# Taps as matmuls, the skip term by scaled copies and flips, B and C of the first half chunk by matmuls, a new table of places

## The reference

```python
# 1: a state space layer, D_INNER 256, 16 states, 4 taps, rank 8
x_b, z = split(x @ W_in)                        # 256 and 256
xc = silu(conv_b + sum_k xpad[:, k:k + T] * conv_w[:, k])   # causal, 4 taps
proj = xc @ W_xproj                             # 40 columns: 8 delta, 16 B, 16 C
delta = softplus(proj[..., :8] @ W_dt + b_dt)
h = exp(delta * A) * h + delta * B * xc         # A = -exp(A_log), 16 states per channel
y = (sum_s h * C + D_param * xc) * silu(z)      # D_param * xc is the skip term
x = layernorm(x + y @ W_out)
# 2: retention between x (queries) and the context (keys, values)
x = layernorm(x + ((rot(x Wq) rot(ctx Wk)^T) * decay_mask) (ctx Wv))
# 3: 16 experts of 64 hidden units, the best 2 of each token, and a shared expert of 128
combine = softmax over the top 2 of (x @ router_w.T + router_bias), 0 elsewhere
x = layernorm(x + sum_e combine_e * (silu(x gate_e) * (x up_e)) down_e + shared(x))
```

## Time and profile before

| | |
|---|---|
| median of 3 runs | 1159.82 us (1152.06 to 1161.8) |
| the profiled execution | 1162.05 us, span of its instructions 1160.2 |
| mean granted TensorE clock | 0.965 of full |
| VectorE busy | 1064.0 (92%), 1492 instructions |
| TensorE busy | 1059.0 (91%), its weight loads 741.8 (64%) |
| ScalarE busy | 994.5 (86%) |
| GpSimd busy | 971.1 (84%) |
| largest groups | products with C 604.0, scans 595.3 on VectorE, decays 424.8, drives 328.4 |

### The profile page before, as it was taken

One profiled execution on the slowest core, in us unless ns is written; L12 is line 12 of the kernel. 1 busy time (PEld: TensorE's weight loads), 2 busy tenths in 40 slices (PEclk: granted clock), 3 DMA queues, 4 the chain that ended last, 5 costly groups with the idle time before them and its releaser, 6 DMA issues. The chain is left out here.

```text
span 1160.2 us, 18257 instructions
## 1 busy us (share of the span) xinstructions
PE 1059.0 (91%) x5831; PEld 741.8 (64%) x5831; DVE 1064.0 (92%) x1492; ACT 994.5 (86%) x2176; POOL 971.1 (84%) x590
## 2 busy tenths in 40 slices
PE   5677888999999999999999989999999999899998
PEld 2455665666767666666666657666666667666665
DVE  2999999999999999999999979999999999999532
ACT  5888898999989898999989879898999989898443
POOL 0587788989989898898989869898989988898844
PEclk9787999999999999999999989999999999999899
DMA  6543543555565544555554364554555655444212
GB/s 165 209 175 138 178 172 130 174 188 190 182 205 178 178 154 156 187 212 192 185 180 145 135 186 179 183 186 163 169 175 186 211 192 166 168 154 157 82 69 74
DMA packets 84111, 194.49 MB, mean 168 GB/s; under 512 B 17288, under 2 KB 47936, under 8 KB 67632
## 3 DMA queue, kind: packets, MB, share of 16 engines
q1 hardware_dynamic: 84016, 193.33, 48.8%
HBM read 179.14 MB, written 5.77 MB: 159 GB/s over the span
## 5 line engine op out<-in xcount | busy, mean ns | idle before, releaser
L934 POOL TENSOR_TENSOR read<-state,bc_all 128x1024 f32<-128x1024 f32 x256 | 604.0, 2363 | 130.4 <-DVE state L804 109.6
L804 DVE TENSOR_TENSOR_SCAN state<-decay,drive_bank 128x512 f32<-128x512 f32 (+1 forms) x464 | 595.3, 1315 | 0.4
L754 ACT ACTIVATE decay<-delta,a_neg 128x252 f32<-128x252 f32 x1024 | 424.8, 494 | 0.9
L796 DVE TENSOR_TENSOR drive_bank<-dx_bank,bc_all 128x512 f32<-128x512 f32 (+1 forms) x496 | 328.4, 701 | 3.3 <-issue 2.3
L371 PE MATMUL y_bank<-ident,read 128*128 128x128 f32 x2048 | 279.2, 281 | 30.9 <-POOL read L934 30.8
L371 PEld LDWEIGHTS y_bank<-ident,read 128*128 128x128 f32 x2048 | 240.1, 145 | 101.6 <-POOL read L934 58.1
L973 POOL TENSOR_TENSOR hid<-gu,comb_all 128x512 f32<-128x512 f32 (+1 forms) x136 | 164.8, 1212 | 17.3 <-DVE gu L895 13.8
L362 PEld LDWEIGHTS down_bank<-down_w,hid 128*128 128x128 f32 x1024 | 129.4, 192 | 38.3 <-issue 30.0
L362 PE MATMUL bank<-x2T,gate_w 128*128 128x512 f32 (+1 forms) x272 | 139.0, 603 | 9.4 <-ACT delta L734 3.9
L362 PE MATMUL down_bank<-down_w,hid 128*128 128x128 f32 x1024 | 134.9, 277 | 2.6 <-POOL hid L973 0.7
L362 PE MATMUL bank<-x2T,up_w 128*128 128x512 f32 (+1 forms) x272 | 132.9, 582 | 0.8 <-ACT xc L710 0.7
(11 more groups left out here) (128 smaller groups left out, 1384.7 us busy)
## 6 DMA issues: line engine op xcount, KB each, us to landing
bc_all<-bc_dram SPq DMA_DIRECT2D x128, 1024.0 KB, 5.4
comb_all<-comb_dram SPq DMA_DIRECT2D x240, 128.0 KB, 3.0
x_in<-in_x_dram SPq DMA_DIRECT2D x15, 256.0 KB, 5.7
ctx_in<-in_ctx_dram SPq DMA_DIRECT2D x15, 256.0 KB, 6.3
k_pair<-k_pair SPq DMA_DIRECT2D x30, 128.0 KB, 2.1
q_pair<-q_pair SPq DMA_DIRECT2D x30, 128.0 KB, 2.5
out_dram<-y_out SPq DMA_DIRECT2D x15, 256.0 KB, 3.1
comb_all<-comb_dram SPq DMA_DIRECT2D x32, 64.0 KB, 2.6
```

Source lines behind the costliest of these rows:

```text
L754: done = e.activation(seqs(decay_t[j % DECAYS][:, i, h, :])[:, :, 1:T], seqs(delta[c % 2][:, h, sub * SUB:(sub + 1) * SUB])[:, :, 1:T], AC ...
L796: e.tensor_tensor(drive_bank[:, a:b, :, :], dx_bank[:, :, :].unsqueeze(1).to_broadcast(shape), bc_all[group % BC_BUFS][:, 0, PAIR * i + a: ...
L804: e.tensor_tensor_scan(states(state_t[j % STATE_BUFS], a, b), states(decay_t[j % DECAYS], a, b), states(drive_bank, a, b), 0.0, ALU.mult, ...
L934: e.tensor_tensor(read_t[j % READS][:, :, :, :], state_t[j % STATE_BUFS][:, :, :, :], bc_all[group % BC_BUFS][:, 1, PAIR * i:PAIR * (i + 1 ...
```

## The change

What it does, part by part:

- Both halves of the convolution are four tap matmuls each, followed by silu with the bias (`xc`). The projection of half 1, the conv pass on ScalarE and the three taps on VectorE go. `w_tap` is made for both halves, from tap rows spread over all partitions (512 KB instead of 256).
- The skip term: ScalarE copies xc, scaled by D_param per channel, to `xd`, and TensorE adds it to `y_bank` by four transposes against the identity. `d_diag` goes.
- The weights W_dt are padded with zero rows from 8 to 40, so that delta is made from all 40 rows of `proj`.
- The first group of B and C is spread over the partitions by TensorE, a column of the identity repeated as weights, into `down_bank` and `y_bank`, and copied to `bc_all` by VectorE. The other groups go through DRAM as before.
- Start: the loads are spread over the queues of SyncE, ScalarE and GpSimd, many constants are loaded later, three activations on one column load function tables ahead of their use, `a_neg` is made on ScalarE, and for the first chunk VectorE copies `proj` and makes `dx_bank`.
- Last chunk: the combine weights are spread by 8 matmuls with a selector matrix, which VectorE makes behind its last scan, into `drive_bank`, `dx_bank` and `y_bank`; VectorE instead of GpSimd multiplies `hid`.
- `AT` and `EXP_AT` have five columns, for the first two chunks, the middle ones, the last but one and the last, and all places are new. `WHOLE_DRIVES` has four entries instead of one, `WHOLE_SCANS` four instead of three.

The diff, cut to its core:

```diff
+COLUMN = [3, 4] + [0] * (CHUNKS - 4) + [2, 1]
...
-    "tap_mm": [(-38, -40)],
-    "xb_mm": [(-43, -41)],
...
+    "weight_mm": [
+        (17, 129, -8, 6, 21), (12, 133, 11, 11, 1), (16, 133, -7, -21, 1), (14, 135, 17, 11, 4),
+        (12, 135, -7, -21, 1), (18, 135, -6, -1, 4), (2, 135, -7, 6, 11), (12, 135, -6, 6, -2)],
...
+    "tap_mm": [(-42, -40, -40, -61, -42), (-38, -38, -36, -46, -36)],
+    "xc": [(-36, -35, -36, -28, -44), (-34, -32, -32, -25, -43)],
+    "xd": [(1, 3, -7, -4, 3), (32, 25, 25, -1, 39)],
 }
-WHOLE_DRIVES = (7,)
-WHOLE_SCANS = (3, 6, 14)
+WHOLE_DRIVES = (3, 7, 8, 9)
+WHOLE_SCANS = (6, 7, 8, 9)
...
+        def last_weight(pair):
+
+            if pair < PAIR * HALVES:
+                return drive_bank[:, pair // HALVES, pair % HALVES, :]
+            return dx_bank[:, pair % HALVES, :] if pair < PAIR * HALVES + 2 else y_bank[:, pair % HALVES, :]
...
+                for c, h in due(tick, "tap_mm"):
+                    bank = take(("xb", c, h), tick, 3)
                     w.wait_ge(S["xT"], at(c))
-                    w.wait_ge(S["w_tap"], 1)
+                    w.wait_ge(S["w_tap"], h + 1)
                     for n in range(TAPS):
-                        done = mm(seqs(bank.t[:, 0:width(c)])[:, :, n:T], w_tap[:, TAPS - 1 - n, :],
+                        done = mm(seqs(bank.t[:, 0:width(c)])[:, :, n:T], w_tap[:, h, TAPS - 1 - n, :],
                                   seqs(xT[c % 3][:, 0:width(c)])[:, :, 0:T - n], start=n == 0, stop=n == TAPS - 1)
                     done.then_inc(S["tap_mm"], 1)
-                    bank.free = (S["xc"], at(c, 0, HALVES))
-                for c in due(tick, "xb_mm"):
-                    bank = take(("xb", c, 1), tick, 6)
...
+                    bank.free = (S["xc"], at(c, h, HALVES))
...
+                    if c == 0:
+                        for two in (0, 1):
+                            for pair in (0, 1):
+                                w.wait_ge(S["bc_copy"], 2 * two + pair - 1)
+                                for i in range(PAIR):
+                                    row = DT_RANK + GROUP * pair + PAIR * two + i
+                                    done = mm((down_bank, y_flat)[pair][:, i * SUB:(i + 1) * SUB],
+                                              ident[0:PROJ, row:row + 1].to_broadcast([PROJ, P]), proj[0:PROJ, 0:SUB])
+                                done.then_inc(S["bc_mm"], 1)
...
+                    mm(last_weight(pair), selector[0:EXPERTS, pair * P:(pair + 1) * P],
+                       combT[:, 0:SUB]).then_inc(S["weight_mm"], 1)
...
-                                mm(y_bank[:, q, h * P:(h + 1) * P], xc[c % 2][:, h, cols], d_diag[:, h, :],
-                                   start=h == 0 and q == 0, stop=False)
+                                flip(y_bank[:, q, h * P:(h + 1) * P], xd[:, h, q * P:(q + 1) * P],
+                                     start=h == 0 and q == 0, stop=False)
...
-                for c in due(tick, "conv_bias"):
-                    w.wait_ge(S["xb_mm"], at(c))
-                    w.wait_ge(S["xc"], at(c - 1, 1, HALVES))
-                    e.activation(conv[:, 0:width(c)], bank_of["xb", c, 1][:, 0:width(c)], ACT.Identity, bias=conv_b[:, 1:2],
-                                 scale=conv_w[:, 1, TAPS - 1:TAPS]).then_inc(S["conv_bias"], 1)
...
+                for c, sub in due(tick, "xd"):
+                    w.wait_ge(S["d_consts"], 16 * 2)
+                    w.wait_ge(S["xc"], at(c, 1, HALVES))
+                    w.wait_ge(S["y"], steps_before(c) + SUB_STEPS * (sub - 1) + 1)
+                    for h in range(HALVES):
+                        done = e.activation(xd[:, h, :], xc[c % 2][:, h, sub * SUB:(sub + 1) * SUB], ACT.Copy,
+                                            scale=d_param[:, h:h + 1])
+                    done.then_inc(S["xd"], 1)
...
-                for c in due(tick, "tap1"):
-                    tap(c, 1)
-                for c in due(tick, "tap2"):
-                    tap(c, 2)
-                for c in due(tick, "tap3"):
-                    tap(c, 3)
...
+                for c, pair in due(tick, "hid"):
+                    if c < LAST:
+                        continue
...
+                    e.tensor_tensor(hid[index % 3][:, 0:SUB], gu[index % 2][:, 0:SUB], last_weight(pair),
+                                    ALU.mult).then_inc(S["last_hid"], 1)
...
-            e.dma_start(tap_rows, io["L0_attn_conv_w"][0:P, :].rearrange(
-                "n k -> (n k)").unsqueeze(0).to_broadcast([P, P * TAPS])).then_inc(first, 16)
...
+            e.dma_start(tap_rows, io["L0_attn_conv_w"].rearrange(
+                "n k -> (n k)").unsqueeze(0).to_broadcast([P, INNER * TAPS])).then_inc(S["tap_consts"], 16)
```

425 lines of the change are left out of this document (242 added, 183 removed), and 5 rows, old and new, of the table EXP_AT.

## The result

The changed kernel is slower by some 2%: median 1174.16 us (1173.02 to 1175.18, 4 runs) against 1157.49 (1152.06 to 1161.8) of the kernel before, a ratio of 1.0192 (95% interval 1.016 to 1.0224). Forecast was 1134. The profiled run has a span of 1173.4, 13.2 more than before.

What follows compares the result with a forecast made beforehand. VectorE was taken as the bound, TensorE only 2.76 us behind. Span: 1160.2 - 9 (start) - 6.3 (first periods) - 12.6 (steady chunks) + 2 (end) = 1134.3; against the median 1134, own range 1125 to 1143.

Steps and rivals of the forecast that it cites:

- TensorE in a steady chunk: Middle chunks: added taps less projection and skip-term records give net +1.6 us, busy 62.98 to 64.6, taken as the bound.
- rival 2: TensorE's 2.76 us idle per chunk stays: 1150 with half of it, 1166 with all; chance 0.16.
- VectorE's saving: Steady chunk: three taps gone (1.91 us) and fewer split drives and scans (0.20) lower VectorE's load by 2.11.
- The same by place: Second reckoning, by order within a steady chunk: TensorE's sum about 1.2 us later, VectorE stands 1.1 and keeps 1.0.
- The place at 358.66: VectorE's scan needing its state buffer back from GpSimd's product; VectorE had 2.14 us in hand there.
- Rival 1: TensorE isn't the bound, weight loads being busy 67%: twelve chunks keep 2.11 us, time 1121 or 1114; chance 0.24.
- Rival 3: Half clock on TensorE without slack costs more chunks: three more eat the gain, six more give 1189; chance 0.07.
- The first chunks: First three chunk periods: later stages' work partly absent, so VectorE's full 2.11 us counts in each, 6.3 gained.
- The start: Up to the first drive: taps start at 8.2, clock rises inside them, drive at 21.4 instead of 30.37, gain 9.
- The end: Last sum of reads to the end: 3.4 us more TensorE matmuls, 1.4 of waits gone, +2 net, between -2 and +4.
- ScalarE's copies: Four scaled copies a chunk at 0.39 us each, 1.6 together, hidden by VectorE's work; unhidden, 19 in all, 1153.

## Why the prediction was wrong

**TensorE in a steady chunk: work right, bound wrong.** Busy 64.6 was forecast and 64.51 measured; ScalarE 60.2 and 60.14; VectorE 63.6 and 64.41. The failed step is "Taken as a bound, a chunk then takes 64.6". That took TensorE's 2.76 of idle time in the earlier trace rows for slack that added work would fill. TensorE stood as long as before, and the chunk took 62.98 + 1.6 + 2.76 = 67.3, measured 67.26. This is rival 2 at its full price; it had 0.16, with 1150 at half of the pauses and 1166 at all of them. Against the forecast that is 67.3 - 64.65 = 2.6 a chunk, 31 in the twelve. That TensorE's work counts in full in the changed kernel is shown: less two taps, 1.65 of 1.68 came back. Why the idle time stayed is shown in part. The pause for the logits is the same one, and issuing the logits earlier only moved it. But the 1.1 for GpSimd's product did go, as the forecast would have it, and 1.16 for two copies by ScalarE came; that the sum is the same to 0.01 is luck. What puts these two copies late in the new table no run took apart. The changed kernel with the old skip term, without ScalarE's scaled copies, wasn't run.

**VectorE's saving** was mis-sized: 2.11 was forecast, 65.53 to 64.41 is 1.12. (65.53 - 2.11 would be 63.4; the 63.6 comes from the chunk's 65.74.) The taps alone spared it 1.42, where 1.91 was counted.

**The same by place.** That both ways agreed was no second proof. The place at 358.66 was reckoned by how late one sum would be. But in the changed kernel TensorE has no pause through fifty microseconds around it, so a sum is as late as all the work since the last pause makes it, not only the records between two sums.

**Rival 1.** The Trainium skill, "Perfetto Trace Analysis", section "Identifying the Most-Contended Engine", takes weight loads' busy share, with the arithmetic done as a share of the peak, as the better sign of TensorE's headroom. Here the share is 66%, and the run with two taps fewer decides against reading the rest as slack: each record left out shortened the chunk.

**Rival 3, the clock, went the other way.** The forecast's terms left the half-clock stretches as they were. They went. The sum of the twelve periods is then 12.6 forecast as gain, 31 not gained, 16.7 got back from the clock and 1.5 from the last two periods (67.07 and 65.77): about 0. The reason given against this rival, "a fuller TensorE stands less", isn't what the runs show: TensorE stands as long as before, and with two taps fewer, at 62.90 busy against 62.98 in the kernel before, eleven of the twelve periods still ran at 1.00. With the taps of half 1 back on VectorE TensorE has least to do of all runs, 88% of the span, and its mean clock is 0.973; the lowest, 0.948, is that of the skip term alone, at 91%. So it isn't the sum of TensorE's work that decides; what in the order does stays open. The Trainium skill's words on transposes ("TensorE: Matmul & The Clock Gate", Part 4) can't be tested here: every middle chunk of the changed kernel with the new flips ran at 1.00, but in the kernel before the flips alone came with a lower clock, and ScalarE's lateness came with them.

**The first chunks.** Forecast was -6.3, counted as if VectorE's saving came in full; measured +13.5, the largest miss beside the steady chunk. The prediction put the new places of chunk 0 at nothing, and "not all the work of the later stages is there" was a reason to expect gain only if their order leaves TensorE free. With the old places of that chunk 8.6 came back. With two taps fewer nothing came back here, so this loss is one of waits and half clock, not of TensorE's added taps. How touchy these periods are shows in the run with the earlier logits, which leaves chunk 0 as it is: 198.8. The rest isn't taken apart.

**The start.** The first drive came at 24.18, not 21.4. Timeline of TensorE there, the counterpart of the earlier trace rows:

```profile
9.82 5.02 PE L392 MATMUL bank<-xT,w_tap 128*128 128x256 f32 x16 [5.58 <-DVE w_tap L835]
...
15.44 1.03 PE L392 MATMUL bank<-xc,w_xproj 128*40 128x256 f32 x4 [0.17 <-ACT xc L768]
...
17.95 1.02 PE L392 MATMUL down_bank<-proj,ident 40*128 40x256 f32 x4
18.81 1.23 PE L392 MATMUL y_bank<-proj,ident 40*128 40x256 f32 x4
19.84 1.98 PE L392 MATMUL down_bank<-proj,ident 40*128 40x256 f32 x4
21.62 1.91 PE L392 MATMUL y_bank<-proj,ident 40*128 40x256 f32 x4
```

The records did get faster in the taps, as put: w_xproj took 1.03, not 1.93. (The half level before is read from the length of the records; the granted clock of the trace reads 1.00 from 6 to 30 there, and from 6 to 18 now.) But the taps start at 9.82 instead of 8.2, because VectorE can start on the rows at 8.61, and could at 6.85 before; whether the double size or the new order of the loads does that isn't shown. After two short pauses, 0.17 and 0.51, the granted clock is 0.50 from 20 to 24, and the last two broadcasts cost 0.9 more each. Of the 6.2, 3.0 were lost before the first cut. Timeline of VectorE there, after, then before, and of GpSimd after:

```profile
38.86 1.64 DVE L908 TENSOR_SCALAR row_mean<-row_sum 128x2 f32<-128x2 f32 x1
40.54 2.40 DVE L912 TENSOR_TENSOR w_qkv<-w_qkv,row_mean 128x128 f32<-128x128 f32 x1
```

```profile
36.26 0.17 DVE L834 TENSOR_SCALAR row_mean<-row_sum 128x2 f32<-128x2 f32 x1
36.47 0.29 DVE L838 TENSOR_TENSOR w_qkv<-w_qkv,row_mean 128x128 f32<-128x128 f32 x1
```

```profile
38.12 4.68 POOL L1027 TENSOR_TENSOR read<-state,bc_all 128x1024 f32<-128x1024 f32 x2 [4.21 <-PE y_bank L401]
```

Two small operations, 0.46 together before, take 4.04, a loss of 3.6. Beside them lie GpSimd's two products of 38.12 to 42.80; before, they lay between the first product, which ends at 36.33, and the second, from 39.28, but for 0.07.

**The end** was +2.8 for +2 forecast; its single terms weren't separated.

**ScalarE's copies** took 0.50 each (502 ns, mean of 64), not the 0.39 of the silu of that shape. ScalarE's busy time came out as forecast; whether the copies are hidden in the changed kernel no run tells, and they have 1% of its chain that ended last. In the kernel before they were not hidden.

No version that ran is faster than the kernel before. Beside the one with two taps left out, the best are the two with old places in the first chunks, 1.0137 (1.0091 to 1.0184) and 1.0141 (1.011 to 1.0173).

## What to carry to other kernels

Idle time of an engine that issues in order is slack only if the waits would shorten. Where they don't, added work can cost its full time even with another engine busier on the page. Before moving work from the busiest engine, sum work and waits for each engine that receives, leave a little of its work out to see what comes back, and read the first and the last chunks by their own rows. A table of places is one piece: moving one stage alters which buffer the next ones get.

## What the runs showed of the hardware

- A VectorE operation on SBUF operands can stand for what is left of a GpSimd operation beside it: 2.20 instead of 0.66 for 128x512, 2.40 instead of 0.29 for 128x128, 1.64 instead of 0.17 for 128x2. The Trainium skill, "SBUF — State Buffer", section "Who interferes with whom", says that only the pair of ports which the two engines share causes contention, as an exclusive lock, and that a VectorE instruction with two SBUF inputs contends with a GpSimd instruction that reads SBUF. The trace agrees: the 2.40 begins at 40.54 and ends at 42.94, GpSimd's second product ends at 42.80.
- TensorE's share of busy time didn't tell its granted clock: all middle chunks with 62.6 busy of 67.57 ran at 1.00 (taps on VectorE), and chunks with 65.5 of 69.2 at 0.95 (skip term alone). Pauses of 1.11 and 1.09 at the same place were followed by half clock once and once not.
